# Three PSUM banks for the tiles of the maxima; keys, values and queries share the bank of the turned tiles

## The chip, the cores and the metric

The kernel runs on one core of one Trainium2 chip. The metric is the device time of that core in microseconds (us), the median of several runs. The engines that matter are TensorE (PE in the profile; its weight loads are PEld), VectorE (DVE), ScalarE (ACT), GpSimd (POOL) and SyncE (SP), which here only issues DMAs. PSUM is used as 8 banks of 128 x 512 float32.

## The reference

Cut to what matters; all in float32, B=16 sequences of 128 tokens, D=512.

```python
Q = (layernorm(x) @ Wq + bq)      # 16 heads of 32
K = ctx @ Wk + bk                 # ctx: 2048 x 512 for each sequence, ONE key head of 32
V = ctx @ Wv + bv                 # and one value head of 32
x = x + softmax(Q K^T / sqrt(32)) V @ Wo + bo
x = x + delta_rule_attention(layernorm(x))   # 4 heads of 128, chunks of 64, Ww, Wr, decay
x = x + top1_experts(layernorm(x))           # 16 experts, w1 512x2048, relu, w2 2048x512
```

## The kernel before

The program has two parts. `attention` does the first two lines of work and the routing for all sequences; `experts` then runs the 16 experts. The change is in `attention` alone.

**Iterations and ticks.** `attention` is a pipeline over sequences, with an order written by hand. All engines run the same loop, `for i in range(-1, B + 1): for t in range(TICKS)`, with 128 ticks an iteration. In iteration i, sequence i is scored, sequence i+1 is prepared (`prepare`: normalise x, turn the context, project keys, values and queries) and sequence i-1 is finished (`finish`: output projection, the delta rule with its 6 levels, routing). A tick is no time: it only fixes the program order on each engine. Each engine runs its list strictly in that order, and semaphores tie the lists together. Within a tick PE does the score, then `prepare`, then the weighted sums, then a tile of the maxima, then `finish`; DVE does `prepare`, maxima, `finish`; ACT does the exponential, `prepare`, `finish`.

**The work of an iteration on PE.** A score tile (L370) on every even tick goes to one of two banks, and ACT turns it into weights (L553). The maxima that the softmax subtracts are found ahead, a head group g at a time: 16 tiles (`largest`, L357), each reduced by DVE (L708), then DVE forms the negated maxima (L715), PE turns them (`turn_max`, L362) and ACT copies the row out (L559, `mrow`). The weighted sums are L382. POOL adds up the weights (L917, 15 for each of 4 groups, 60 an iteration), and at tick 9 of the next iteration `sums` (L396) reduces those. From them DVE forms reciprocals (L764) and the attention output `turned` (L767), which the output projection (L336 with wo) waits for at tick 15.

**The work of `prepare`.** DVE takes the statistics of x (L722, L704, at tick NORM), POOL the reciprocal root (L920, L922, same tick), DVE normalises into xin (L727, at tick XN), PE turns xin (L332, at tick XNT), ACT copies it out (L570). 16 tiles of the context are turned by PE (L332, ticks TILE_AT) and copied out by ACT (L582, into cxT, which the trace calls w_first). After every fourth comes the projection of keys and values (L437, ticks KV_AT); ACT copies one half (L589, kvlow), DVE adds the other (L743, kvs) one tick later, ACT rounds the keys (L596) two ticks later, DVE takes the rest (L749). The values are turned at VT_AT. The queries are projected at ticks QPROJ to QPROJ+3 (L414), scaled by DVE (L733), rounded by ACT (L575), the rest taken by POOL (L930), and SP sends them to their place with 12 DMAs of 64 KB (L288, at tick QSEND). The first tile of the maxima of the next sequence (tick 89) waits for all 12.

**Banks.** A_BANK: two for the tiles of the maxima. B_BANK: two for scores. PV_BANK: weighted sums. T_BANK: turned x, context tiles and values. KV_BANK: keys and values, queries, and half of `sums`. P_BANK: `finish`. A use of a bank waits until the use before it has been read.

```python
NORM, XN, XNT, QPROJ, QSEND = 1, 5, 10, 27, 38
TILE_AT = [8 + 4 * k for k in range(KB)]      # 8, 12, ..., 68
MAX_AT, MAX_TURN = [15 * n // 8 - 39 for n in range(KB)], -8   # from tick 32 g of its own iteration
```

Of the kernel before, what the change touches and what calls it, by code (L numbers as in the profile page):

```python
# [9 lines left out]
P = 128  # L10
# [27 lines left out]
NORM, XN, XNT, QPROJ, QSEND = 1, 5, 10, 27, 38  # L38
TILE_AT = [8 + 4 * k for k in range(KB)]
KV_AT = [TILE_AT[4 * c + 3] + 3 for c in range(4)]  # L40
VT_AT = [KV_AT[2 * m + 1] + 7 for m in range(2)]
# [60 lines left out]
def attention(nc, T, w1_first, w1_in):  # L102
    with ExitStack() as ctx:
# [10 lines left out]
        A_BANK, B_BANK, PV_BANK, T_BANK, KV_BANK, P_BANK = bank[0:2], bank[2:4], bank[4], bank[5], bank[6], bank[7]  # L114
# [86 lines left out]
        def level(b, lv, part=0):  # L201
# [6 lines left out]
            [(XNT, ("x", 0))] + [(t, ("t", k)) for k, t in enumerate(TILE_AT)]  # L208
            + [(t, ("v", c)) for c, t in enumerate(VT_AT)])]

# [3 lines left out]
        def turn_read(b, use):  # L214
# [27 lines left out]
        def banks_of(b):  # L242

            return [P_BANK] if b < LAST else [P_BANK, KV_BANK, T_BANK, PV_BANK]
# [81 lines left out]
        def _(e):  # L326
# [33 lines left out]
            def turn_max(b, g):  # L360
                e.wait_ge(*mneg_dve.at(b, g))
                e.transpose(A_BANK[(17 * g + 16) % 2][:, 0:P], mneg[:], ident).then_inc(a_pe.sem, 1)  # L362
# [10 lines left out]
            def weigh(b, u):  # L373
# [3 lines left out]
                if k == 0 and (b or g):  # L377
                    e.wait_ge(*(oS_act.at(b, g - 1) if g else oS_act.at(b - 1, HG - 1)))
# [7 lines left out]
            def sums(b):  # L386
# [12 lines left out]
            def prepare(b, t):  # L399
# [6 lines left out]
                if t == QPROJ:  # L406
                    if b == 0:
                        e.wait_ge(*wq_in.at(0))
                    e.wait_ge(*kvs_dve.at(b, 0))
                    e.wait_ge(*xnT_act.at(b))  # L410
                if QPROJ <= t < QPROJ + HG:
                    cols = slice((t - QPROJ) * P, (t - QPROJ + 1) * P)
                    for c in range(DC):
                        ins = e.matmul(KV_BANK[:, cols], wq[:, c, cols], xnT[:, c, :], start=c == 0, stop=c == DC - 1)  # L414
# [811 lines left out]
```

## Time and profile before

| what | value |
|---|---|
| runs shown | 2424.21 us median of 3 (2420.67 to 2426.93) |
| profiled execution, its own time | 2427.98 us |
| its span (first to last instruction) | 2426.1 us |
| mean granted TensorE clock in it | 0.946 of full speed |
| busy, share of the span | PE 90%, PEld 59%, DVE 57%, ACT 49%, POOL 68% |
| iterations 1 to 14 (with `prepare` and `finish` both) | sums (L396) at 1000.90, 1118.05 and 1236.43 us: 117.8 us apart on average |
| first tile of the maxima | 53.7 us |
| experts | from about 1990 us to the end |

The profile is of one execution, so sums are made against its own time; it lies 3.8 us above the median. An engine's row gives start, duration, engine and line; what stands in square brackets is how long the engine sat idle before, and what ended the idle time. PE records overlap: a matmul's duration includes the draining of the array, so what an instruction costs PE is read from start to next start. Line numbers are those of the kernel before.

### The profile page before, as it was taken

To read this page: it belongs to the slowest core of one execution; us is meant where nothing else is said; L and a number is where in the kernel's file an instruction comes from. 1 tells how busy PE (TensorE), PEld (TensorE's weight loads), DVE (VectorE), ACT (ScalarE), POOL (GpSimd) and SP (SyncE) were. 2 spreads that over 40 slices of the span, in tenths; PEclk is the share of its full clock that TensorE was granted. 3 is DMA by queue.
4 is the path that set the end of the run, shared out by engine and by line. 5 is a ranking of instruction groups with operands and counts; after the bars stand their busy time and mean duration, and the time that the engine had idled before them with its cause. 6 is when DMAs were issued, how large, how long until landed. Compare 5 with 4: busy or idle time off the path is not lost. (4 is left out here: it accounts for less than half of the span.)

```text
span 2426.1 us, 35019 instructions
## 1 busy us (share of the span) xinstructions
PE 2189.4 (90%) x12608; PEld 1429.9 (59%) x12608; DVE 1371.0 (57%) x2311; ACT 1193.3 (49%) x2237; POOL 1638.2 (68%) x1323
## 2 busy tenths in 40 slices
PE   5889898989998989898989898989898769999999
PEld 3435555546464646464646464645554448999998
DVE  2665757566667566666666666666665433333333
ACT  3555554646464646464645455555554313333333
POOL 0676878677777777777777777777777714655655
PEclk9889998999899989998999899989998889999999
DMA  4532120202020202121211111121120009999995
GB/s 160 188 113 66 40 82 24 83 23 83 23 83 23 83 26 80 40 66 40 66 47 58 51 59 63 43 66 42 59 79 9 18 14 375 350 363 346 362 363 189
DMA packets 108157, 263.75 MB, mean 109 GB/s; under 512 B 9849, under 2 KB 35065, under 8 KB 99792
## 3 DMA queue, kind: packets, MB, share of 16 engines
q1 hardware_dynamic: 98448, 235.32, 27.7%
q10 hardware_dynamic: 5952, 14.29, 1.6%
q0 software_dynamic: 3584, 11.90, 1.2%
q8 instruction: 101, 1.65, 0.3%
q14 instruction: 72, 0.59, 0.1%
HBM read 223.74 MB, written 25.72 MB: 103 GB/s over the span
## 5 line engine op out<-in xcount | busy, mean ns | idle before, releaser
L917 POOL TENSOR_TENSOR psum<-psum,p 128x512 f32<-128x512 f32 x896 | 1162.9, 1298 | 291.7 <-ACT p L553 197.7
L708 DVE TENSOR_REDUCE mpart<-bank 128x1 f32<-128x512 f32 x1024 | 675.0, 682 | 403.5 <-PE bank L357 396.1
L553 ACT ACTIVATE p<-bank 128x512 f32<-128x512 f32 x1024 | 596.8, 600 | 553.5 <-PE bank L370 543.6
L357 PE MATMUL bank<-kT,qT 96*128 96x512 f32 x1024 | 484.1, 480 | 62.6 <-DVE mpart L708 32.5
L370 PE MATMUL bank<-qT,kT 97*128 97x512 f32 x1024 | 502.4, 492 | 4.7 <-ACT p L553 4.0
L357 PEld LDWEIGHTS bank<-kT,qT 96*128 96x128 f32 x1024 | 199.6, 196 | 211.5 <-DVE mpart L708 104.6
L370 PEld LDWEIGHTS bank<-qT,kT 97*128 97x128 f32 x1024 | 201.7, 197 | 142.6 <-issue 113.6
L382 PE MATMUL bank<-p,v 128*32 128x512 f32 x2048 | 271.4, 651 | 0.0
L1159 POOL TENSOR_TENSOR w2l<-w,w2h 128x1024 fp32r<-128x1024 f32 x64 | 203.2, 3177 | 75.1 <-PE ebank L1074 54.4
L332 PE MATMUL bank<-cst,w_first 128*128 128x128 f32 x1024 | 164.1, 287 | 21.7 <-DMA w_first<-in_ctx 18.0
L332 PEld LDWEIGHTS bank<-cst,w_first 128*128 128x128 f32 x1024 | 134.3, 149 | 64.9 <-issue 29.4
L917 POOL TENSOR_TENSOR psum<-p 128x512 f32<-128x512 f32 x64 | 81.8, 1278 | 122.5 <-ACT p L553 101.6
L582 ACT COPY w_first<-bank 128x512 f32<-128x512 f32 x256 | 149.3, 586 | 15.0 <-PE bank L332 14.9
L1102 ACT ACTIVATE hh<-ebank 128x512 fp32r<-128x512 f32 x64 | 38.3, 599 | 225.3 <-PE ebank L1058 225.3
L1096 ACT CAST w2h<-w 128x2048 fp32r<-128x2048 f32 x64 | 121.5, 1898 | 44.1 <-DMA w<-in_w 44.1
L382 PEld LDWEIGHTS bank<-p,v 128*32 128x32 f32 x2048 | 56.7, 116 | 141.7 <-issue 107.3
L437 PE MATMUL bank<-w_first,wkv 128*64 128x512 f32 x512 | 125.7, 612 | 10.0 <-ACT w_first L582 9.8
L336 PE MATMUL bank<-wo,turned 128*128 128x512 f32 x128 | 90.3, 799 | 38.8 <-DVE turned L767 38.8
L1058 PE MATMUL ebank<-dT,w_first 128*128 128x128 f32 x1024 | 120.9, 279 | 0.9 <-DVE dT L1117 0.9
L1058 PEld LDWEIGHTS ebank<-dT,w_first 128*128 128x128 f32 x1024 | 120.0, 195 | 2.4 <-issue 1.2
L1123 DVE TENSOR_TENSOR w2l<-w,w2h 128x1024 fp32r<-128x1024 f32 x64 | 79.1, 1236 | 71.9 <-PE ebank L1074 48.0
L1128 DVE SCALAR_TENSOR_TENSOR hl<-ebank,hh 128x512 fp32r<-128x512 f32 x64 | 44.2, 691 | 133.4 <-ACT hh L1102 133.4
(159 smaller groups left out, 3137.8 us busy)
## 6 DMA issues: line engine op xcount, KB each, us to landing
w<-in_w SPq DMA_DIRECT2D x48, 2048.0 KB, 20.1
w_first<-in_ctx SPq DMA_DIRECT2D x64, 1024.0 KB, 4.9
w_first<-in_w SPq DMA_DIRECT2D x16, 2048.0 KB, 11.6
dispatched<-route ACTq DMA_DIRECT2D x17, 513.0 KB, 4.4
dis<-dispatched SPq DMA_DIRECT2D x16, 513.0 KB, 3.5
qT<-qh SPq DMA_DIRECT2D x128, 64.0 KB, 2.0
xin<-in_x SPq DMA_DIRECT2D x16, 256.0 KB, 2.6
qT<-qs SPq DMA_DIRECT2D x64, 64.0 KB, 2.0
```

The source lines that it names most:

```text
L332: ins = e.transpose(out[0:m, j * P:(j + 1) * P], src(j), ident)
L357: e.matmul(a[:], qT[b % 2][0:3 * HD, (4 * g + h) * P:(4 * g + h + 1) * P], kT[b % 2][0:3 * HD, c * 512:(c + 1) * 512], start=True, stop=Tr ...
L370: e.matmul(B_BANK[u % 2][:], kT[b % 2][0:3 * HD + 1, k * P:(k + 1) * P], qT[b % 2][0:3 * HD + 1, g * 512:(g + 1) * 512], start=True, stop= ...
L382: ins = e.matmul(PV_BANK[HD * j:HD * (j + 1), :], v1[b % 2][:, k + j, :], p[(UNITS * b + u + j) % NP][:], start=k == 0, stop=k == KB - 4)
L437: ins = e.matmul(KV_BANK[rows, :], wkv[:, j, :], cxT[c % 2][:, j, :], start=j < 2, stop=j >= 2)
L553: e.activation(p[n % NP][:], B_BANK[u % 2][:], ACT.Exp).then_inc(p_act.sem, 1)
L582: e.copy(cxT[c % 2][:, :, kk * P:(kk + 1) * P], turn_bank(b, ("t", k))[:].rearrange("p (c t) -> p c t", c=DC)).then_inc(cxT_act.sem, 1)
L708: e.tensor_reduce(mpart[g % 2][:, n:n + 1], A_BANK[(17 * g + n) % 2][:], AX.X, ALU.max).then_inc(max_dve.sem, 1)
L917: e.tensor_tensor(acc[:], first[:], p[(UNITS * b + u) % NP][:], ALU.add).then_inc(psum_pool.sem, 1)
L1058: ins = e.matmul(H_BANK[g][:, f * P:(f + 1) * P], w1[q][:, c, (4 * g + f) * P:(4 * g + f + 1) * P], dT[q][:, c, :], start=c == 0, stop=c = ...
L1096: e.copy(w2h[g][:], w2[q][:, 4 * g:4 * g + 4, :]).then_inc(w2h_act.sem, 1)
L1159: e.tensor_tensor(w2l[g % 2][:, 2:4, :], w2[q][:, 4 * g + 2:4 * g + 4, :], w2h[g][:, 2:4, :].bitcast(F32), ALU.subtract).then_inc(w2l_pool ...
```

## The change

KV_BANK is given up: A_BANK gets its bank as a third one, and all that used KV_BANK in `prepare` now takes its turn in T_BANK. `sums` puts its reciprocal half into PV_BANK. `turn_read` gives the wait for the use before. Since T_BANK now has 24 uses an iteration in place of 19, the ticks are laid out anew: context tiles at 9, 12, 15, 18, then 25, 28, 31, 34, and so on up to 66, keys and values at 21, 37, 53, 69, queries at 72 to 75, values at 78 and 81.

```diff
-NORM, XN, XNT, QPROJ, QSEND = 1, 5, 10, 27, 38
-TILE_AT = [8 + 4 * k for k in range(KB)]
+NORM, XN, XNT, QPROJ, QSEND = 0, 3, 6, 72, 82
+TILE_AT = [9 + 16 * (k // 4) + 3 * (k % 4) for k in range(KB)]
 KV_AT = [TILE_AT[4 * c + 3] + 3 for c in range(4)]
-VT_AT = [KV_AT[2 * m + 1] + 7 for m in range(2)]
+VT_AT = [78, 81]
-        A_BANK, B_BANK, PV_BANK, T_BANK, KV_BANK, P_BANK = bank[0:2], bank[2:4], bank[4], bank[5], bank[6], bank[7]
+        A_BANK, B_BANK, PV_BANK, T_BANK, P_BANK = bank[0:3], bank[3:5], bank[5], bank[6], bank[7]
             [(XNT, ("x", 0))] + [(t, ("t", k)) for k, t in enumerate(TILE_AT)]
+            + [(t, ("k", c)) for c, t in enumerate(KV_AT)] + [(QPROJ, ("q", 0))]
             + [(t, ("v", c)) for c, t in enumerate(VT_AT)])]
+            if kind == "q":
+                return q_dve.at(b)
+            if kind == "k":
+                return kvs_dve.at(b, i)
+        def a_bank(b, g, n):
+            return A_BANK[(17 * (4 * b + g) + n) % 3]
             def largest(b, g, n):
-                a = A_BANK[(17 * g + n) % 2]
-                if n >= 2:
-                    e.wait_ge(*max_dve.at(b, 16 * g + n - 2))
-                elif n == 0 and 64 * b + 16 * g >= 1:
-                    e.wait_ge(*max_dve.at(0, 64 * b + 16 * g - 1))
-                elif n == 1 and 4 * b + g >= 1:
-                    e.wait_ge(*mrow_act.at(0, 4 * b + g - 1))
+                group = 4 * b + g
+                a = a_bank(b, g, n)
+                if n >= 3:
+                    e.wait_ge(*max_dve.at(b, 16 * g + n - 3))
+                elif n == 2 and group:
+                    e.wait_ge(*mrow_act.at(0, group - 1))
+                elif group:
+                    e.wait_ge(*max_dve.at(0, 16 * group - 2 + n))
             def weigh(b, u):
-                    e.wait_ge(*(oS_act.at(b, g - 1) if g else oS_act.at(b - 1, HG - 1)))
+                    e.wait_ge(*(oS_act.at(b, g - 1) if g else o_dve.at(b - 1, "recip3")))
             def sums(b):
-                if b + 1 < B:
-                    e.wait_ge(*kvs_dve.at(b + 1, 3))
-                for out, lhs, src in ((KV_BANK, cst[:, C_ONES, 0:HD], psum), (P_BANK, cst[:, C_STACK, 0:HD], oS)):
+                for out, lhs, src in ((PV_BANK, cst[:, C_ONES, 0:HD], psum), (P_BANK, cst[:, C_STACK, 0:HD], oS)):
             def prepare(b, t):
                 if t == QPROJ:
-                    e.wait_ge(*kvs_dve.at(b, 0))
+                    e.wait_ge(*turn_read(b, ("q", 0)))
                 if t in KV_AT:
-                    if c:
-                        e.wait_ge(*kvs_dve.at(b, c - 1))
-                    elif b:
-                        e.wait_ge(*(o_dve.at(b - 2, "recip3") if b > 1 else kvs_dve.at(0, 3)))
-                    if c == 1:
-                        e.wait_ge(*q_dve.at(b))
+                    e.wait_ge(*turn_read(b, ("k", c)))
```

Line numbers below are, for each kernel, its own; L340, L366, L379, L403, L344 and L391 after the change are L332, L357, L370, L396, L336 and L382 before it.

The first place is PE from tick 4 to tick 12 of an iteration, where x is turned (`cst,xin`) and `sums` stands (psum and oS). Before:

```order
L370 MATMUL bank<-qT,kT 128x512
L357 MATMUL bank<-kT,qT 128x512
L370 MATMUL bank<-qT,kT 128x512
L332 MATMUL bank<-cst,w_first 128x128 x4
L357 MATMUL bank<-kT,qT 128x512
L396 MATMUL bank<-psum,cst 32x512 x4
L396 MATMUL bank<-oS,cst 32x512 x4
L357 MATMUL bank<-kT,qT 128x512
L370 MATMUL bank<-qT,kT 128x512
L332 MATMUL bank<-cst,xin 128x128 x4
```

And in the changed kernel, from the score of tick 6:

```order
L379 MATMUL bank<-qT,kT 128x512
L340 MATMUL bank<-cst,xin 128x128 x4
L366 MATMUL bank<-kT,qT 128x512
L379 MATMUL bank<-qT,kT 128x512
L366 MATMUL bank<-kT,qT 128x512
L340 MATMUL bank<-cst,w_first 128x128 x4
L403 MATMUL bank<-psum,cst 32x512 x4
L403 MATMUL bank<-oS,cst 32x512 x4
L366 MATMUL bank<-kT,qT 128x512
```

The turning of x, which stood behind `sums`, now stands ahead of it, and the first context tile directly before `sums`.

The second place is ACT after the first projection of keys and values (kvlow is its copy), up to the copy of the second context tile behind it. Before:

```order
L589 COPY kvlow<-bank 64x512
L611 ACTIVATE rk,ss<-xn 128x128 x4
L553 ACTIVATE p<-bank 128x512
L582 COPY w_first<-bank 128x4x128
L559 CAST mrow<-bank 4x128
L596 CAST kT<-kvs 32x512 x2
L620 COPY turned<-bank 128x512
L553 ACTIVATE p<-bank 128x512
L617 ACTIVATE rk<-xn,rn 128x128 x4
```

In the changed kernel:

```order
L591 COPY kvlow<-bank 64x512
L555 ACTIVATE p<-bank 128x512
L598 CAST kT<-kvs 32x512 x2
L613 ACTIVATE rk,ss<-xn 128x128 x4
L555 ACTIVATE p<-bank 128x512
L561 CAST mrow<-bank 4x128
L584 COPY w_first<-bank 128x4x128
L622 COPY turned<-bank 128x512
L555 ACTIVATE p<-bank 128x512
L619 ACTIVATE rk<-xn,rn 128x128 x4
```

The two casts of the keys, which wait for kvs, now stand ahead of the squares, of an exponential, of the row of maxima and of the tile's copy.

The third place is SP over one iteration: the rows of maxima (mrow), the context loads and the queries (qh, qs). Before:

```order
L279 DMA qT<-mrow 1x4x128
L270 DMA w_first<-in_ctx 128x2048
L288 DMA qT<-qh 32x4x128 x8
L288 DMA qT<-qs 32x4x128 x4
L270 DMA w_first<-in_ctx 128x2048
L279 DMA qT<-mrow 1x4x128
L270 DMA w_first<-in_ctx 128x2048 x2
L279 DMA qT<-mrow 1x4x128
```

In the changed kernel:

```order
L287 DMA qT<-mrow 1x4x128
L278 DMA w_first<-in_ctx 128x2048 x2
L287 DMA qT<-mrow 1x4x128
L278 DMA w_first<-in_ctx 128x2048 x2
L296 DMA qT<-qh 32x4x128 x8
L296 DMA qT<-qs 32x4x128 x4
L287 DMA qT<-mrow 1x4x128
```

The 12 sends have moved from behind the first of the four rows of maxima to directly ahead of the third.

## Rows read from the trace of the kernel before

**Rows 1.** The page: engines, and the costliest groups (mean ns of one after busy us).

```profile
PE 2189.4 (90%) x12608; PEld 1429.9 (59%) x12608; DVE 1371.0 (57%) x2311; ACT 1193.3 (49%) x2237; POOL 1638.2 (68%) x1323
...
L708 DVE TENSOR_REDUCE mpart<-bank 128x1 f32<-128x512 f32 x1024 | 675.0, 682 | 403.5 <-PE bank L357 396.1
L553 ACT ACTIVATE p<-bank 128x512 f32<-128x512 f32 x1024 | 596.8, 600 | 553.5 <-PE bank L370 543.6
```

**Rows 2.** Waits of PE, 12 iterations (409 to 1813 us): total us, times, longest.

```profile
PE bank L336 <- DVE turned L767: 27.7, 12, 2.3
PE bank L357 <- ACT mrow L559: 21.6, 23, 1.2
PE bank L357 <- DVE mpart L708: 20.9, 36, 0.7
...
PE bank L332 <- ACT w_first L582: 5.5, 12, 0.5
```

**Rows 3.** Timeline around `sums` of one iteration: start, duration, [idle before <-releaser].

```profile
1115.47 1.29 POOL L917 TENSOR_TENSOR psum<-psum,p 128x512 f32<-128x512 f32 x1
...
1116.33 0.51 PE L370 MATMUL bank<-qT,kT 97*128 97x512 f32 x1
...
1116.98 0.57 POOL L922 TENSOR_TENSOR rs<-rs,mhalf 128x1 f32<-128x1 f32 x1
...
1117.58 1.52 DVE L727 TENSOR_SCALAR xin<-xin,mv,rs 128x512 f32<-128x512 f32 x1 [0.33 <-POOL rs L922]
...
1118.05 1.07 PE L396 MATMUL bank<-psum,cst 128*32 128x512 f32 x8
...
1120.48 0.60 PE L332 MATMUL bank<-cst,xin 128*128 128x128 f32 x4
...
1121.81 0.66 PE L332 MATMUL bank<-cst,w_first 128*128 128x128 f32 x4 [0.25 <-ACT xnT L570]
...
1126.21 2.07 PE L336 MATMUL bank<-wo,turned 128*128 128x512 f32 x2 [2.31 <-DVE turned L767]
```

**Rows 4.** Windows of 4 us there: busy us of each engine, then PE's granted clock.

```profile
1122.00:1126.00 4.00, 1.42 (x7) 0.68 (x6) 4.00 (x6) 1.34 (x3) 3.39 (x3) 0.91 0.23 68
1126.00:1130.00 4.00, 3.79 (x8) 2.25 (x9) 0.76 (x2) 1.00 (x2) 3.60 (x3) 0.50 0.00 0
```

**Rows 5.** Timeline from the first projection of keys and values, one iteration.

```profile
1019.25 1.94 PE L437 MATMUL bank<-w_first,wkv 128*64 128x512 f32 x8 [0.26 <-ACT w_first L582]
...
1021.23 0.59 ACT L589 COPY kvlow<-bank 64x512 f32<-64x512 f32 x1 [1.54 <-PE bank L437]
...
1021.86 0.74 DVE L743 SCALAR_TENSOR_TENSOR kvs<-bank,bkv,kvlow 64x512 f32<-64x512 f32 x1
...
1023.06 0.60 ACT L553 ACTIVATE p<-bank 128x512 f32<-128x512 f32 x1
...
1024.18 1.25 ACT L596 CAST kT<-kvs 32x512 fp32r<-32x512 f32 x2
...
1024.32 0.49 PE L357 MATMUL bank<-kT,qT 96*128 96x512 f32 x1 [1.24 <-ACT mrow L559]
...
1024.65 1.05 PE L414 MATMUL bank<-xnT,wq 128*128 128x128 f32 x8
...
1026.68 0.60 PE L332 MATMUL bank<-cst,w_first 128*128 128x128 f32 x4
```

**Rows 6.** Sending the queries, its landing, and PE at ticks 76 and 89.

```profile
1032.66 5.21 SPq L288 DMA_DIRECT2D qT<-qh  x8
...
DMA to landing us min/median/max: 2.0/2.0/2.1
...
1072.41 0.39 PE L370 MATMUL bank<-qT,kT 97*128 97x512 f32 x1
...
1082.49 0.47 PE L357 MATMUL bank<-kT,qT 96*128 96x512 f32 x1
```

**Rows 7.** Timeline of the start: the first tile of the maxima.

```profile
53.71 1.19 PE L357 MATMUL bank<-kT,qT 96*128 96x512 f32 x2 [1.44 <-DVE kT L749]
```

More of the change, by code:

```diff
@@ L242, in banks_of @@
         def banks_of(b):
-            return [P_BANK] if b < LAST else [P_BANK, KV_BANK, T_BANK, PV_BANK]
+            return [P_BANK] if b < LAST else [P_BANK, A_BANK[2], T_BANK, PV_BANK]
         block = ctx.enter_context(nc.Block())
@@ L361, in turn_max @@
                 e.wait_ge(*mneg_dve.at(b, g))
-                e.transpose(A_BANK[(17 * g + 16) % 2][:, 0:P], mneg[:], ident).then_inc(a_pe.sem, 1)
+                e.transpose(a_bank(b, g, 16)[:, 0:P], mneg[:], ident).then_inc(a_pe.sem, 1)
             def score(b, u):
@@ L413, in prepare @@
                     for c in range(DC):
-                        ins = e.matmul(KV_BANK[:, cols], wq[:, c, cols], xnT[:, c, :], start=c == 0, stop=c == DC - 1)
+                        ins = e.matmul(turn_bank(b, ("q", 0))[:, cols], wq[:, c, cols], xnT[:, c, :], start=c == 0, stop=c == DC - 1)
                     if t == QPROJ + HG - 1:
@@ L428, in prepare @@
                     e.wait_ge(*cxT_act.at(b, 4 * c + 3))
-                    if c:
-                        e.wait_ge(*kvs_dve.at(b, c - 1))
-                    elif b:
-                        e.wait_ge(*(o_dve.at(b - 2, "recip3") if b > 1 else kvs_dve.at(0, 3)))
-                    if c == 1:
-                        e.wait_ge(*q_dve.at(b))
+                    e.wait_ge(*turn_read(b, ("k", c)))
                     for j in range(DC):
                         rows = slice(64 * (j % 2), 64 * (j % 2) + 2 * HD)
-                        ins = e.matmul(KV_BANK[rows, :], wkv[:, j, :], cxT[c % 2][:, j, :], start=j < 2, stop=j >= 2)
+                        ins = e.matmul(turn_bank(b, ("k", c))[rows, :], wkv[:, j, :], cxT[c % 2][:, j, :], start=j < 2, stop=j >= 2)
                     ins.then_inc(kv_pe.sem, 1)
@@ L558, in max_row @@
                     e.wait_ge(*(mrow_in[g - 2].at(b) if g >= 2 else mrow_in[g + 2].at(b - 1)))
-                e.copy(mrow[g % 2][:], A_BANK[(17 * g + 16) % 2][0:4, 0:P]).then_inc(mrow_act.sem, 1)
+                e.copy(mrow[g % 2][:], a_bank(b, g, 16)[0:4, 0:P]).then_inc(mrow_act.sem, 1)
             def out_sum(b, g):
@@ L588, in prepare @@
                         e.wait_ge(*(kvs_dve.at(b, c - 1) if c else kvs_dve.at(b - 1, 3)))
-                    e.copy(kvlow[half(c), :], KV_BANK[half(c + 1), :]).then_inc(kvlow_act.sem, 1)
+                    e.copy(kvlow[half(c), :], turn_bank(b, ("k", c))[half(c + 1), :]).then_inc(kvlow_act.sem, 1)
                 if t - 2 in KV_AT:
@@ L707, in largest @@
                 e.wait_ge(*a_pe.at(b, 17 * g + n))
-                e.tensor_reduce(mpart[g % 2][:, n:n + 1], A_BANK[(17 * g + n) % 2][:], AX.X, ALU.max).then_inc(
+                e.tensor_reduce(mpart[g % 2][:, n:n + 1], a_bank(b, g, n)[:], AX.X, ALU.max).then_inc(
                     max_dve.sem, 1)
@@ L732, in prepare @@
                         e.wait_ge(*q_in.at(b - 1, 11))
-                    e.scalar_tensor_tensor(heads(qs[:]), heads(KV_BANK[:]), SCALE,
+                    e.scalar_tensor_tensor(heads(qs[:]), heads(turn_bank(b, ("q", 0))[:]), SCALE,
                                            bq[:].unsqueeze(2).to_broadcast([P, DC, P]), ALU.mult, ALU.add).then_inc(
@@ L742, in prepare @@
                         e.wait_ge(*kl_dve.at(b - 1, c + 1))
-                    e.scalar_tensor_tensor(kvs[c // 2][half(c), :], KV_BANK[half(c), :], bkv[half(c), 0:1],
+                    e.scalar_tensor_tensor(kvs[c // 2][half(c), :], turn_bank(b, ("k", c))[half(c), :], bkv[half(c), 0:1],
                                            kvlow[half(c), :], ALU.add, ALU.add).then_inc(kvs_dve.sem, 1)
@@ L763, in finish @@
                     e.wait_ge(*sums_pe.at(b))
-                    e.reciprocal(cut(recip, h), cut(KV_BANK, h)).then_inc(o_dve.sem, 1)
+                    e.reciprocal(cut(recip, h), cut(PV_BANK, h)).then_inc(o_dve.sem, 1)
                 if t == POST["att"]:
```

## The prediction

> **What bounds the kernel now.** I read the page first. PE is busy 90% of the span, no other engine much over two thirds [rows 1], so outside the experts' part time goes where PE waits. The waits of PE over 12 like iterations come next [rows 2]: 27.7 us for `turned` at tick 15, 21.6 us for the row of maxima (mrow), 20.9 us for DVE's reductions (mpart), 5.5 us for the copies of context tiles (w_first). The change can touch the last three, 48.0 us, 4.0 us an iteration; over the 14 iterations with all their work that is 56 us.
>
> Then I read the timeline to see what ends each wait, because a wait of PE is worth its length only if nothing else ends just behind it. Around `sums` it is a chain through four engines [rows 3]: POOL adds its last weights (1115.47), only then makes the reciprocal root for the next sequence's x (1116.98 to 1117.55), DVE normalises x (1117.58 to 1119.10), and PE turns it at 1120.48, 1.4 us after it is ready and 2.4 us behind `sums`. From `sums` (1118.05) a second chain runs through DVE's reciprocals to `turned`, and PE meets it after 2.31 us of idling, at 1126.21. So every tile that PE could do earlier between tick 0 and tick 15 only lengthens that idle time. In the middle of the iteration, behind the first projection of keys and values, PE idles 1.24 us for mrow [rows 5].
>
> **The change, part by part.** All sums are for one iteration from 1 to 14.
>
> *x is turned before `sums` (XNT 10 to 6).* This is the largest term. PE reaches tick 6 at 1116.33 [rows 3], and its score takes some 0.4 us, so it would turn x at about 1116.7. What it turns is ready at 1119.10. NORM and XN are only one and two ticks earlier; POOL's root still stands behind its last addition, and DVE waits for that root already (0.33 us), so xin comes no earlier. PE therefore stands about 2.4 us, and as its list is strict, `sums` stands behind it. From x to `sums` the new list has x, a maxima tile, a score, a maxima tile and context tile 0. x with one tile and one score took 1121.81 - 1120.48 - 0.25 = 1.08 us [rows 3]; for the other two I take 0.7 (an estimate: two of the same three kinds). `sums` starts at 1119.15 + 1.78 = 1120.9, not 1118.05: +2.85, and `turned` follows by as much. If DVE's saved idle moments bring POOL's last addition forward, this falls to about 2.1, and I keep that as the low end. I take +2.8.
>
> *The clock around it.* After the idle time that ends at 1126.21 the granted clock falls from 0.91 of a window to 0.50, which is the lower of the two levels, 1.2 GHz [rows 4]. The new stand before `sums` is about as long, so `sums` and the tiles may run at that level: its two halves take about 1.85 us at full speed (an estimate: two records like the one of 1.07 us, a little overlapped [rows 3]), so up to +1.9. Nothing shows whether the fall lands on them; I take +0.8 and keep 0 and 1.9. The Trainium skill (TensorE: Matmul & The Clock Gate, Part 1: The HAM clock gate) says the low level is the default and activity lifts it; by it a stand can only cost clock. The trace agrees, with 0.50 behind the 2.31 us stand.
>
> *A context tile hidden.* The tile of tick 16 moves to 15, ahead of the wait for `turned`, where PE is idle anyway. A tile is a part of the 1.08 us above, about 0.4, and up to twice that in the slow stretch. I take -0.6.
>
> *Keys and values in the turn bank, first group (23 to 21).* Two things meet here. The last maxima tile of the group now stands behind the projection, so DVE reduces it and forms mneg before it takes kvs; and ACT casts the keys, which wait for kvs, ahead of all else (second place in the change). From the projection's start: 1.9 until the maxima tile, 0.55 until DVE starts, 0.68 reduction, 0.25 for mneg, 0.74 kvs [rows 1, 5]: 4.1 us. Then on ACT the casts 1.25, the squares 1.25 (from 1021.82 to 1023.06), an exponential 0.60, mrow 0.25, the tile's copy 0.6, in all 4.0 [rows 1, 5]. Only then is the bank free for the second context tile: 8.2 us behind the projection's start. Before it took 1026.68 - 1019.25 = 7.43 us to the like tile, with 1.24 of waiting for mrow and with two blocks of queries (0.8 each from 1024.65 [rows 5]) that now go elsewhere, and without one score of 0.3: like for like 6.1. That is +2.1, less the 0.26 waited ahead of the projection, +1.9. So the wait for mrow goes, and a longer one for kvs and ACT's copies comes. Low end 0.3, if ACT is less loaded than my sum; I take +1.9. The Trainium skill (TensorE: Matmul & The Clock Gate, Architectural detail) says ScalarE's queue is strictly first in, first out, TensorE alone pulling weight loads ahead. Were it otherwise, the copy could pass casts and squares and the term would be about -0.6; by the rule the term stands, and rows 5 agree (kvlow, exponential, casts in the list's order).
>
> *The rest of the middle.* Removed: a wait for mpart and one for a copy, about 0.6 and 0.5 with refilling 0.3, together -1.4 [rows 2]. Added: tiles that share one bank 3 ticks apart. A tile may follow 1.33 us behind the one before (1120.48 to 1121.81 [rows 3]); where the three ticks hold nothing of `finish`, PE's own work between is about as long, and ACT's 0.60 exponentials and 1.25 casts lie between. I count six such places an iteration at 0.2 to 0.3 each, 1.5, and 0.2 before the queries. Together +0.3, between -1.4 and +1.5.
>
> *Queries late (27 to 72, sent at 82).* SP needs 5.21 us for 8 sends, so 7.8 for 12, and the last lands 2.0 behind its issue [rows 6]: 9.2 us from the first. DVE's scaling and ACT's rounding come ahead, 1.5 us. Needed: 10.7 from the end of the projection. PE's list from tick 76 to 89 took 1082.49 - 1072.41 = 10.08 us [rows 6], plus 0.4 for the values now at 81, less 0.2 of drain: 10.3. So the first maxima tile waits 0.4. What is queued behind it on PE is everything, scores too. If the sends land later, each us counts in full. I take +0.4, between 0 and 1.5.
>
> *At no cost.* The 16 matmuls of the queries are only moved. The new wait of the weighted sums for the reciprocals at tick 17 lies behind `turned`, which PE has met at 15. mrow at tick 121: its 0.61 us lies directly before a wait for routing, so PE just waits there longer. The mpart waits between ticks 2 and 13 vanish into the stand for x and for `turned`.
>
> **Sum.** 2.8 + 0.8 - 0.6 + 1.9 + 0.3 + 0.4 = +5.6 us an iteration, 78 over 14. The start: before the first maxima tile at 53.7 [rows 7] the queries no longer hide under context loads, perhaps +5 for projecting and sending 12 pieces behind the last keys, less 2 as the first group goes at DVE's 0.68 a tile; iteration 0 and the last save perhaps 4 us of maxima waits. Net about -2 with rounding, +-6. 2428 + 76 = 2504 for an execution like the profiled one, and 3.8 less beside the median: **2500 us**.
>
> **The rivals.**
>
> *Only the stand for x costs.* The middle's new waits are fully paid by the removed ones (1.9 + 0.3 becomes 0, no clock, queries just in time). 14 x 2.8 = 39: 2463. For it: ACT is idle a good part of the time on average, so its lag may be smaller. Against it: rows 5 show ACT and DVE in unbroken work exactly there.
>
> *The clock takes more.* Two stands an iteration of over 2 us (x, and the keys' group with 3.4 us in pieces) each bring a stretch at 1.2 GHz; a further 2 us an iteration, the price of a doubled `sums`, 28 us: 2530. This is the rule named above, at work once more. For it: rows 4. Against it: the wait of 1.24 us did not bring one, so short pieces may not.
>
> *It is faster.* One mechanism: xin is ready when PE reaches tick 6. It decides if POOL's root comes 2.4 us earlier, which needs POOL's last additions that much earlier; then three banks give what they promise in the middle, the waits for mrow and mpart and copies go (1.24 + 0.6 + 0.5 with refilling 0.3 each), some 2.7 us an iteration, 38 in all: 2386. Against it: POOL's list has no gap between the additions at that place, and its order there has not changed.
>
> *No net change.* The bank waits save 2.7, the stand costs 2.8: 2424.
>
> **How the numbers follow.** Forecast 0.47, only the stand 0.20, clock 0.18, faster 0.10, no change 0.05. The predicted time is the forecast's. The range: down to 2445 takes in the single stand; up to 2545 takes in the clock and later landings (0.4 becoming 1.5 is 15 us). Left out are faster, no change and tails, about 0.2. Within 0.3% (7 us) a measurement of this kernel could not tell it from no change. Faster by more: 0.10; within: 0.05; slower: 0.85.
>
> **What would show it.** Right: `sums` rows lie about 123 us apart; PE waits for DVE xin (after the change it is the first reason at the turning of x) some 2.4 us, 14 times; mrow is gone from the list of PE's waits; waits for kvs and for copies of w_first have grown to 2 to 4 us an iteration; a small wait for the DMA of queries at the first maxima tile. Wrong: x turned at once after tick 6's score, or the second context tile less than 7 us behind the first projection. The prediction fails most likely if DVE and POOL run earlier against PE than here: their lead is measured in this order of the work, and a PE that stands more leaves them more time.

## The result, and the profile after

The changed kernel takes 2559.2 us (median of 4 runs, 2548.2 to 2562.5); the kernel before took 2422.7 us beside it (median of 4). The ratio is 1.055 [1.053, 1.058]: 136.5 us slower, where +76 was forecast. The sign and the two places of the new waits were as forecast, the size was outside the range of 2445 to 2545.

The profiled execution of the changed kernel has a time of 2559.62 us of its own. Its page answers to [rows 1]:

```profile
span 2557.8 us, 35006 instructions
...
PE 2247.7 (88%) x12608; PEld 1459.1 (57%) x12608; DVE 1378.5 (54%) x2311; ACT 1193.4 (47%) x2237; POOL 1632.9 (64%) x1323
```

The same 12608 matmuls keep PE busy 58 us longer than before (2247.7 against 2189.4) in a span 132 us longer. PE thus both works more slowly and stands more: 58 us of the difference are slower work, 73 us are idle time. Its waits from 409 to 1813 us, the stretch of [rows 2], now hold 11 iterations (total us, times, longest):

```profile
PE bank L340 <- DVE xin L729: 36.2, 11, 3.7
PE bank L344 <- DVE turned L769: 33.3, 11, 3.0
PE bank L515 <- DVE oh L832: 20.5, 11, 1.9
PE bank L366 <- issue: 20.4, 11, 2.3
PE bank L371 <- DVE mneg L717: 6.5, 11, 0.6
PE bank L379 <- ACT p L555: 6.5, 20, 0.7
PE bank L366 <- DVE mpart L710: 6.3, 16, 0.4
PE bank L340 <- DVE kvs L745: 6.3, 11, 0.9
```

The wait for mrow is gone, that for mpart fell from 20.9 to 6.3 us, and two new ones stand for them: 3.3 us an iteration for x, 1.9 us at the first maxima tile. Together the two new ones are 56.6 us here, more than the 42.5 us that mrow and mpart had. The wait for routing (`oh`, L515) has grown too, from 10.9 to 20.5 us: PE comes there earlier, but `oh` does not, so that part of what the third bank saves is lost again (with the maxima on two banks, below, this wait is 10.6).

Now the same stretch as windows, of the kernel before (first) and of the changed one (second): busy us of PE, PEld, DVE, ACT and POOL, then the granted clock.

```profile
409.00:1813.00 1404.00, 1291.09 (x7269) 769.42 (x7268) 904.77 (x1540) 769.10 (x1557) 1045.40 (x906) 0.96 0.17 56
```
```profile
409.00:1813.00 1404.00, 1248.40 (x6734) 734.65 (x6732) 848.86 (x1442) 712.38 (x1439) 968.60 (x844) 0.92 0.16 50
```

The clock fell from 0.96 to 0.92. As there are only the levels 0.5 and 1.0, 16% of the stretch now ran at the low one and 8% before: some 20 us of each iteration in place of 9. At most half of such time is lost (in the iteration shown next, a maxima tile starts 0.43 us behind a score in the low stretch, at 1067.11, and 0.24 us behind one at 1071.35, at the full clock; and some of the time is idle anyway), so the added low stretches cost up to about 5 us an iteration.

The timeline of the changed kernel around `sums` answers to [rows 3]:

```profile
1063.48 0.57 POOL L924 TENSOR_TENSOR rs<-rs,mhalf 128x1 f32<-128x1 f32 x1
...
1064.08 1.49 DVE L729 TENSOR_SCALAR xin<-xin,mv,rs 128x512 f32<-128x512 f32 x1 [0.91 <-POOL rs L924]
...
1065.62 0.83 PE L340 MATMUL bank<-cst,xin 128*128 128x128 f32 x4 [3.66 <-DVE xin L729]
...
1068.52 1.46 PE L403 MATMUL bank<-psum,cst 128*32 128x512 f32 x8
...
1077.08 2.08 PE L344 MATMUL bank<-wo,turned 128*128 128x512 f32 x2 [3.02 <-DVE turned L769]
```

The chain POOL root, DVE normalising, PE is the predicted one, and `sums` begins 2.90 us behind x (1068.52 - 1065.62), where 1.78 was estimated. The windows there say why the estimate was short (the clock stands behind POOL's busy time):

```profile
1064.00:1067.00 3.00, 1.38 (x6) 1.28 (x7) 2.17 (x3) 0.51 (x1) 1.28 (x2) 0.83 0.00 0
1067.00:1070.00 3.00, 3.00 (x18) 1.30 (x21) 1.30 (x2) 1.26 (x3) 0.00 (x0) 0.60 0.27 93
1070.00:1074.00 4.00, 3.73 (x23) 2.03 (x15) 2.69 (x4) 2.21 (x5) 2.68 (x3) 1.00 0.00 0
1074.00:1077.00 3.00, 0.06 (x1) 0.00 (x0) 3.00 (x6) 0.45 (x1) 2.71 (x3) 0.87 0.00 0
1077.00:1080.00 3.00, 2.92 (x4) 1.51 (x5) 0.62 (x2) 0.38 (x1) 2.42 (x3) 0.50 0.01 3
1080.00:1083.00 3.00, 3.00 (x14) 0.47 (x16) 0.00 (x0) 0.22 (x1) 2.34 (x2) 0.50 0.00 0
```

Around and behind the end of the stand for x the clock is 0.83 and 0.60, over the tiles and the first half of `sums`; it is back at 1.00 by 1070, and the stand for `turned` makes it fall again.

The first group of keys and values answers to [rows 5]:

```profile
1087.23 1.94 PE L439 MATMUL bank<-w_first,wkv 128*64 128x512 f32 x8
...
1090.64 0.74 DVE L745 SCALAR_TENSOR_TENSOR kvs<-bank,bkv,kvlow 64x512 f32<-64x512 f32 x1
...
1091.42 1.26 ACT L598 CAST kT<-kvs 32x512 fp32r<-32x512 f32 x2 [0.94 <-DVE kvs L745]
...
1094.51 0.57 ACT L584 COPY w_first<-bank 128x512 f32<-128x512 f32 x1
...
1095.13 1.11 PE L340 MATMUL bank<-cst,w_first 128*128 128x128 f32 x4
```

From the projection to the second context tile it is 7.90 us (1095.13 - 1087.23), where 8.2 was worked out: kvs, casts, squares, an exponential and the copy one behind the other on DVE and ACT. And the queries, which answer to [rows 6]:

```profile
1147.06 5.20 SPq L296 DMA_DIRECT2D qT<-qh  x8
...
1152.31 2.53 SPq L296 DMA_DIRECT2D qT<-qs  x4
...
1156.34 0.47 PE L366 MATMUL bank<-kT,qT 96*128 96x512 f32 x1 [1.44 <-issue]
```

The sends begin at 1147.06; the last record ends at 1154.84, its send is issued about 0.6 before, and lands 2.0 later, at about 1156.2. PE goes on at 1156.34. So the releaser that the trace calls "issue" is here the queries' DMA: a wait of PE for something that no engine's instruction ends. (In the run with idle time filled, below, the trace names it at the same wait: `DMA qT<-qs`.)

Over 12 like iterations the stretches of PE's list are (means, before and after, in us):

| from, to | before | after |
|---|---|---|
| `sums` to the output projection | 8.16 | 8.85 |
| on to the turning of maxima, tick 24 | 13.41 | 13.03 |
| tick 24 to 56 | 34.26 | 33.51 |
| tick 56 to 88 (after: with the queries) | 26.32 | 29.57 |
| tick 88 to 120 | 22.66 | 25.20 |
| tick 120 to routing | 2.85 | 2.84 |
| routing to the next `sums` | 10.08 | 13.97 |
| whole iteration | 117.74 | 126.97 |

The iteration grew by 9.2 us, where 5.6 was summed: 3.9 of it around x (that stretch now also holds the turning of x itself), 2.5 from tick 88, where the queries are waited for, and 2.5 from tick 24 to 88.

The same can be split into slower work and idle time. The 14 iterations from the first `sums` to the fifteenth hold the same matmuls in both kernels (8509 and 8506 records). Before they took 1649.8 us (174.36 to 1824.17), PE busy 1517.2; after 1770.1 us (186.63 to 1956.70), PE busy 1573.5. So over all 14 an iteration grew by 8.6 us: 4.0 of slower work and 4.6 of idle time. The rest of the 132 us is the start: the first `sums` comes 12.3 us later than before. From the fifteenth `sums` to the end both take the same (601.9 and 601.1 us).

### The profile page after: what moved, and what is told of

Same layout as the page of the kernel before. It is cut to its first block and busy times, and to the rows that moved or that the text cites. A ratio compares the mean times of both kernels' runs of the same rounds, so it can differ in the third digit from the quotient of the medians.

```text
span 2557.8 us, 35006 instructions
## 1 busy us (share of the span) xinstructions
PE 2247.7 (88%) x12608; PEld 1459.1 (57%) x12608; DVE 1378.5 (54%) x2311; ACT 1193.4 (47%) x2237; POOL 1632.9 (64%) x1323
## 5 line engine op out<-in xcount | busy, mean ns | idle before, releaser
L366 PE MATMUL bank<-kT,qT 96*128 96x512 f32 x1024 | 490.8, 483 | 48.9 <-issue 26.6
L379 PE MATMUL bank<-qT,kT 97*128 97x512 f32 x1024 | 513.2, 507 | 13.5 <-ACT p L555 12.3
L366 PEld LDWEIGHTS bank<-kT,qT 96*128 96x128 f32 x1024 | 211.1, 206 | 195.0 <-issue 122.9
L379 PEld LDWEIGHTS bank<-qT,kT 97*128 97x128 f32 x1024 | 206.9, 204 | 156.1 <-issue 104.3
L391 PE MATMUL bank<-p,v 128*32 128x512 f32 x2048 | 269.4, 647 | 0.0
L340 PE MATMUL bank<-cst,w_first 128*128 128x128 f32 x1024 | 171.5, 296 | 15.1 <-DVE kvs L745 9.8
L340 PEld LDWEIGHTS bank<-cst,w_first 128*128 128x128 f32 x1024 | 130.5, 151 | 68.3 <-issue 32.0
L391 PEld LDWEIGHTS bank<-p,v 128*32 128x32 f32 x2048 | 57.1, 117 | 153.4 <-issue 107.1
L344 PE MATMUL bank<-wo,turned 128*128 128x512 f32 x128 | 94.7, 837 | 50.8 <-DVE turned L769 50.8
L1060 PEld LDWEIGHTS ebank<-dT,w 128*128 128x128 f32 x1024 | 117.5, 192 | 1.4
L1060 PE MATMUL ebank<-dT,w 128*128 128x128 f32 x1024 | 118.2, 275 | 0.0
## 6 DMA issues: line engine op xcount, KB each, us to landing
w_first<-in_w SPq DMA_DIRECT2D x16, 2048.0 KB, 12.3
```

The costliest lines, as they stand in the source:

```text
L340: ins = e.transpose(out[0:m, j * P:(j + 1) * P], src(j), ident)
L366: e.matmul(a[:], qT[b % 2][0:3 * HD, (4 * g + h) * P:(4 * g + h + 1) * P], kT[b % 2][0:3 * HD, c * 512:(c + 1) * 512], start=True, stop=Tr ...
L379: e.matmul(B_BANK[u % 2][:], kT[b % 2][0:3 * HD + 1, k * P:(k + 1) * P], qT[b % 2][0:3 * HD + 1, g * 512:(g + 1) * 512], start=True, stop= ...
L391: ins = e.matmul(PV_BANK[HD * j:HD * (j + 1), :], v1[b % 2][:, k + j, :], p[(UNITS * b + u + j) % NP][:], start=k == 0, stop=k == KB - 4)
L1060: ins = e.matmul(H_BANK[g][:, f * P:(f + 1) * P], w1[q][:, c, (4 * g + f) * P:(4 * g + f + 1) * P], dT[q][:, c, :], start=c == 0, stop=c = ...
```

## The experiments

My theory after the result was that the mechanisms of the prediction hold, but that each stand of PE also costs a stretch at 1.2 GHz, and that the two moves in the order (x ahead, queries late) make nearly the whole loss, not the banks. The rival was that the shared bank, with 24 uses in a row, is what costs: then undoing the moves would give back little. Each kernel was timed in 3 rounds beside the kernel before; ratios are to that kernel. Edits are to the changed kernel unless it is said otherwise. "An iteration" means the difference of the medians divided by 14, so it holds a share of the start too; a table behind the experiments parts the start, the slower work and the idle time.

### x back behind `sums`

```diff
-NORM, XN, XNT, QPROJ, QSEND = 0, 3, 6, 72, 82
+NORM, XN, XNT, QPROJ, QSEND = 1, 5, 10, 72, 82
```

> The changed kernel with NORM, XN, XNT back at 1, 5, 10, all else kept: x is turned behind sums again. Theory (the stand for x ahead of sums, with the slow clock it brings, is the largest part): the wait for xin goes and 4 to 5 us an iteration come back, 2485 to 2505 us. Rival (the bank shared by keys, queries and tiles is the cause): under 1.5 us an iteration comes back, 2535 to 2560.

Measured: 2465.0 us, ratio 1.017 [1.015, 1.019]. That is 94 us less than the changed kernel, 6.7 an iteration, and more than my theory had expected (2485 to 2505). The wait for xin is gone, and the clock in the steady stretch is 0.96 again, as in the kernel before:

```profile
409.00:1813.00 1404.00, 1274.47 (x7113) 753.42 (x7112) 896.91 (x1528) 755.37 (x1532) 1024.81 (x892) 0.96 0.16 53
```

The stand itself had 3.3 us, so another 3.4 an iteration went with it. PE's busy time, with the same 12608 matmuls, says what this is:

```profile
PE 2196.8 (89%) x12608; PEld 1431.7 (58%) x12608; DVE 1375.1 (56%) x2311; ACT 1191.8 (48%) x2237; POOL 1631.9 (66%) x1323
```

The changed kernel has 2247.7 us there. Of the 97.6 us between the two spans (2557.8 and 2460.2) 51 are slower work and 47 are idle time. The slower work I had underrated twice, in the prediction (+0.8) and here.

### Queries early again

```diff
-NORM, XN, XNT, QPROJ, QSEND = 0, 3, 6, 72, 82
-TILE_AT = [9 + 16 * (k // 4) + 3 * (k % 4) for k in range(KB)]
+NORM, XN, XNT, QPROJ, QSEND = 0, 3, 6, 24, 35
+TILE_AT = [(9, 30, 45, 60)[k // 4] + 3 * (k % 4) for k in range(KB)]
```

> The changed kernel with the queries projected at ticks 24 to 27 and sent at 35, and the context tiles behind them moved (30, 33, 36, 39, 45, ...), x still turned at tick 6. Theory (the late queries hold the first maxima tile and bring slow clock): 2 to 2.5 us an iteration come back, 2523 to 2535 us. Rival (the sends are hidden but for 0.4 us, as predicted): at most 8 us in all, 2548 to 2560, and the wait at the first maxima tile was of another cause.

Measured: 2499.6 us, ratio 1.031 [1.029, 1.033]: 60 us less than the changed kernel, 4.3 an iteration, and again more than my theory had expected (2523 to 2535). The wait at the first maxima tile is gone. The context tiles move with it, so this is the price of the queries' place together with that of the tiles around it. It is not the length of that wait: 11.4 us of the gain come ahead of the first `sums`, and in the 14 iterations, 3.4 us shorter each, the idle time is the same (14.0 and 13.9), as waits for kvs, xr and Y have come in its place. What has fallen there is the time at 1.2 GHz, from 19.7 to 14.6 us an iteration, and with it PE's busy time, by 3.3.

### Both back, the banks kept

```diff
-NORM, XN, XNT, QPROJ, QSEND = 0, 3, 6, 72, 82
-TILE_AT = [9 + 16 * (k // 4) + 3 * (k % 4) for k in range(KB)]
+NORM, XN, XNT, QPROJ, QSEND = 1, 5, 10, 24, 35
+TILE_AT = [(9, 30, 45, 60)[k // 4] + 3 * (k % 4) for k in range(KB)]
```

> Both of the above: x turned at tick 10 again, queries at 24 to 27. Theory (the two stands are nearly all of the loss): 2450 to 2475 us if the first group's wait for kvs stays as predicted (1.9 us an iteration), 2420 to 2440 if the queries behind the first projection hide that one too. Rival (shared bank): 2500 or more.

Measured: 2428.9 us, ratio 1.000 [0.999, 1.002]. So with the new banks, x behind `sums` and the queries behind the first projection again, nothing measurable is lost. The single moves give back 94 and 60, both together 130: each is worth less once the other is undone. The rival, that the shared bank makes the loss, has fallen. The time is the one expected for a hidden wait for kvs, but that condition did not come: PE waits 22.4 us for kvs (L421 and L340) in 12 iterations, 1.9 each. The number was luck in that. The new banks are not free either: the 42.5 us of waits for mrow and mpart in [rows 2] are gone, but in the same stretch there are those 22.4 for kvs, and xr has 20.5 where it had 7.8, Y 15.0 where it had 6.3, `oh` 20.5 where it had 10.9.

### The maxima on two banks

```diff
-            return A_BANK[(17 * (4 * b + g) + n) % 3]
+            return A_BANK[(17 * (4 * b + g) + n) % 2]
...
-                if n >= 3:
-                    e.wait_ge(*max_dve.at(b, 16 * g + n - 3))
-                elif n == 2 and group:
-                    e.wait_ge(*mrow_act.at(0, group - 1))
+                if n >= 2:
+                    e.wait_ge(*max_dve.at(b, 16 * g + n - 2))
+                elif n == 0 and group:
+                    e.wait_ge(*max_dve.at(0, 16 * group - 1))
                 elif group:
-                    e.wait_ge(*max_dve.at(0, 16 * group - 2 + n))
+                    e.wait_ge(*mrow_act.at(0, group - 1))
```

> The changed kernel with the tiles of the maxima going round two banks again (the third lies idle), everything else kept. Theory (a third bank buys little, since other waits end just behind): 0 to 2 us an iteration slower than the changed kernel, 2559 to 2590 us. Rival (the third bank is worth the 3 to 4 us an iteration of mpart and mrow waits): 2600 us or more.

Measured: 2588.8 us, ratio 1.067 [1.065, 1.069], 29.6 us more than the changed kernel. The third bank alone is worth 2.1 us an iteration, in a kernel where the stands for x and for queries swallow part of what it saves. The waits from 409 to 1813 us, 11 iterations, show that as well:

```profile
PE bank L366 <- DVE mpart L710: 41.2, 52, 1.2
...
PE bank L366 <- ACT mrow L561: 25.2, 33, 1.6
PE bank L340 <- DVE xin L729: 24.6, 11, 2.3
```

mpart and mrow are back, and the stand for x is 2.2 us an iteration in place of 3.3.

### The old kernel with x early

Here the edit is to the kernel before; its banks and all its other ticks stay.

```diff
-NORM, XN, XNT, QPROJ, QSEND = 1, 5, 10, 27, 38
+NORM, XN, XNT, QPROJ, QSEND = 0, 3, 6, 27, 38
```

> The kernel before with one part of the change alone: NORM, XN, XNT at 0, 3, 6 in place of 1, 5, 10. Banks and all other ticks as before. Theory (the stand for x ahead of sums stems from this part alone and needs no shared bank): 4.5 to 7 us an iteration slower, 2490 to 2520 us, and the clock falls from 0.946 to about 0.925. Rival (it needs the shared bank or the third bank, since these let PE run ahead): under 2450 us.

Measured: 2497.6 us, ratio 1.030 [1.029, 1.032], 74 us more (5.3 an iteration) than the same kernel with x behind `sums`. Its waits from 409 to 1813 us, 12 iterations:

```profile
PE bank L357 <- DVE mpart L708: 38.4, 47, 1.4
PE bank L336 <- DVE turned L767: 27.7, 12, 2.3
PE bank L332 <- DVE xin L727: 24.9, 12, 2.3
```

This tests the first term by itself. The stand is 2.1 us an iteration here, near the 2.4 predicted, and not 3.3: with two banks PE still loses its time to mpart (38.4 us, against 20.9 in [rows 2]) and reaches tick 6 later. In the changed kernel the third bank took those waits away, so PE came to the same chain earlier; the run before, with a stand of 2.2 us on two banks, says that this is what lengthened it. The price is again over the stand's length. Of 4.7 us that the 14 iterations grew by each, 3.2 are idle time, the stand and 1.5 more of waiting for mpart; 1.5 are slower work. The clock in this stretch is 0.93, against 0.96:

```profile
409.00:1813.00 1404.00, 1253.43 (x6888) 737.35 (x6888) 872.50 (x1485) 730.22 (x1479) 999.70 (x871) 0.93 0.16 52
```

### Idle time filled with matmuls that nobody needs

The changed kernel, with 16 more transposes on PE ahead of the wait for x, and 10 ahead of the first maxima tile. Their results are never read; nothing is left out. (The condition on b and the waits on v_act and ohloc keep them off banks that are still read.)

```diff
+                if n == 0 and g == 0 and b:
+                    e.wait_ge(*v_act.at(b, 1))
+                    for _ in range(10):
+                        e.transpose(T_BANK[:, 0:P], ident, ident)
                 if n == 0:
...
+                if t == XNT and b >= 2:
+                    if b >= 3:
+                        e.wait_ge(*post_dve.at(b - 3, "ohloc"))
+                    for _ in range(16):
+                        e.transpose(P_BANK[:, 0:P], ident, ident)
```

> The changed kernel with matmuls added that nobody reads, in the two stands of PE: 16 turnings of the identity into an idle bank directly before the wait for xin (iterations 1 to 14), 10 before the first tile of the maxima of a sequence. At full speed they take about 1.5 and 0.9 us, less than the stands (3.5 and 1.7 us), so they cost nothing there. Theory (part of the loss is the slow clock that the stands bring): the mean clock rises from 0.92 to 0.93 or more and 1 to 3 us an iteration come back, 2515 to 2545 us. Rival (the clock follows something else, the stands cost only their length): clock 0.92, 2555 to 2575 us.

Measured: 2527.6 us, ratio 1.044 [1.041, 1.046]: 31.5 us less than the changed kernel, with more work on PE. Its order is unchanged, and nothing in it makes x come earlier, so I put this down to the clock. Two views show it, the windows around the stand for x:

```profile
1049.00:1052.00 3.00, 1.40 (x13) 1.16 (x11) 2.08 (x3) 0.28 (x1) 2.88 (x4) 1.00 0.44 175
1052.00:1055.00 3.00, 2.62 (x19) 1.58 (x23) 2.14 (x4) 1.67 (x3) 0.00 (x0) 1.00 0.25 87
```

and PE's timeline there:

```profile
1048.82 1.58 PE L415 MATMUL bank<-cst 128*128 128x128 f32 x13
1052.31 0.66 PE L340 MATMUL bank<-cst,xin 128*128 128x128 f32 x4 [1.91 <-DVE xin L738]
...
1054.29 1.06 PE L407 MATMUL bank<-psum,cst 128*32 128x512 f32 x8
```

PE idles 1.91 us and not 3.66, the clock stays at 1.00, and `sums` comes 1.98 us behind x where it came 2.90. Over the 14 iterations the time at 1.2 GHz is 14.1 us each and no longer 19.7. The Trainium skill (TensorE: Matmul & The Clock Gate, Part 1: The HAM clock gate) has activity lifting the clock and idleness dropping it; this run agrees, 0.936 over the span against 0.920. So 2.25 us an iteration is a lower bound of the clock's share at the two places together, since other low stretches remain. The second wait now carries the name of the DMA:

```profile
PE bank L370 <- DMA qT<-qs: 12.1, 11, 2.0
```

### Queries in the middle

```diff
+NORM, XN, XNT, QPROJ, QSEND = 1, 5, 10, 56, 66
+TILE_AT = [(9, 25, 41, 62)[k // 4] + 3 * (k % 4) for k in range(KB)]
```

> The changed kernel with x at tick 10 and the queries at ticks 56 to 59, sent at 66, the last four context tiles behind them (62 to 71). The sends end well before the first tile of the maxima. Theory (only lateness of the queries costs, and as they fill a stretch where PE waits for DVE in the delta rule's levels they may do better than at tick 24): the wait at the first maxima tile is gone, 2405 to 2435 us. Rival (queries at 24 to 27 were good because they cover ACT's and DVE's late work behind the first projection, the 1.9 us of the prediction): 2440 to 2460 us.

Measured: 2447.1 us, ratio 1.009 [1.008, 1.011], 18 us more than with the queries at 24 to 27. The projection is early enough here to be waited for by nobody, and the time is the rival's. The rival's reason is not what the traces show, though: PE idles less here than with the queries at 24 to 27 (9.5 us an iteration against 10.8), so no cover is missed. What is higher is the time at 1.2 GHz, 13.6 us an iteration against 11.0, and PE's busy time, by 2.3 with the same matmuls. Half of what PE works in the added low stretches is 1.3 us an iteration (an estimate), about the size of the whole loss. Why this order has more of such stretches was not tried.

### Keys and values behind the last maxima tile

The first group is spaced so that its projection, three ticks behind the fourth tile, stands behind the last maxima tile of the head group; the later tiles move by one tick.

```diff
+NORM, XN, XNT, QPROJ, QSEND = 1, 5, 10, 25, 36
+TILE_AT = [9, 12, 15, 19] + [(31, 46, 61)[k // 4] + 3 * (k % 4) for k in range(12)]
```

> The kernel with x at tick 10 and early queries (2428.9 us), and the first projection of keys and values moved from tick 21 to 22, so that the last tile of the maxima stands ahead of it on PE and DVE reduces it while the projection runs; queries at 25 to 28, later tiles one tick later. Theory (kvs is late in the first group because DVE takes that reduction and mneg first, 0.85 us): PE's wait for kvs before the queries falls from 1.4 us to under 1, and 0.4 to 0.8 us an iteration come back, 2417 to 2424 us. Rival (kvs waits for kvlow anyway): no change, 2426 to 2432.

Measured: 2403.1 us, ratio 0.992 [0.990, 0.993]: 26 us less than with both moves undone, and more than the 6 to 11 expected. So something else had been moved by the same edit. The next run takes the shift of the later tiles alone:

```diff
+NORM, XN, XNT, QPROJ, QSEND = 1, 5, 10, 24, 35
+TILE_AT = [(9, 31, 46, 61)[k // 4] + 3 * (k % 4) for k in range(KB)]
```

> The kernel with x at 10 and queries at 24 (2428.9 us), whose first projection stays at tick 21, but whose later context tiles stand one tick later (31, 46, 61), as in the kernel that measured 2403.1 us. It parts the two differences of that one. Theory (the gain of 26 us came from DVE's reduction no longer standing ahead of kvs): 2424 to 2432 us here. Rival (it came from where the later tiles stand against the delta rule's levels, whose waits fell from 25 to 10 us): 2403 to 2412 us.

Measured: 2412.0 us, ratio 0.995 [0.993, 0.997]. Of the 26 us, 17 come from the later tiles being one tick later, and 9 from the first projection being behind the last maxima tile, with the queries one tick later. (By the ratios it is 14 and 8, each uncertain by about 6, as the runs were timed beside different runs of the kernel before.) And one more tick:

```diff
+NORM, XN, XNT, QPROJ, QSEND = 1, 5, 10, 25, 36
+TILE_AT = [9, 12, 15, 19] + [(32, 47, 62)[k // 4] + 3 * (k % 4) for k in range(12)]
```

> The kernel of 2403.1 us with its later context tiles one tick later still (32, 47, 62). If the place of the tiles against the levels sets the time, this moves it by more than 5 us either way; if only the first projection does, it stays at 2400 to 2407 us.

Measured: 2396.1 us, ratio 0.988 [0.986, 0.990]. It is the fastest version, 1.2% faster than the kernel before and 6.4% faster than the changed one, with the same banks. Waits of PE from 409 to 1813 us (12 iterations), with both moves undone (first) and in this version (second):

```profile
PE bank L490 <- DVE xr L804: 20.5, 24, 1.5
...
PE bank L421 <- DVE kvs L745: 16.8, 12, 1.7
PE bank L348 <- DVE Y L796: 15.0, 24, 1.0
...
PE bank L340 <- DVE kvs L745: 5.6, 12, 0.5
```
```profile
PE bank L340 <- DVE kvs L745: 15.7, 24, 0.8
PE bank L421 <- DVE kvs L745: 12.2, 12, 1.0
PE bank L490 <- DVE xr L804: 8.8, 24, 0.5
PE bank L340 <- ACT w_first L584: 8.7, 23, 0.5
...
PE bank L348 <- DVE Y L796: 3.7, 12, 0.3
```

The waits inside the delta rule (L490 for xr, L348 for Y) shrank by 23 us: the context tiles now stand where PE waited for DVE between two levels. The waits for kvs (L340) grew by 10. This is the gain of the first tick (there xr has 7.8 and Y 9.2 already). The last tick is not explained by it: Y fell by 5.6 us more, kvs (L340) rose by 7.6, and 2.4 of the 7 us come ahead of the first `sums`.

### All runs, start and iterations

Each row is read from that run's trace. The start is the first row of `sums`; the rest is the mean of the 14 iterations from there to the fifteenth `sums`. All but the filled kernel hold the same matmuls there (8506 to 8509 records), so more busy time means slower work. Idle time is length less busy time. Time at 1.2 GHz is an estimate, 2 x (1 - clock) added up over 400 windows of each trace.

| kernel | start, us | iteration | PE busy | PE idle | at 1.2 GHz |
|---|---|---|---|---|---|
| before | 174.4 | 117.8 | 108.4 | 9.5 | 10.6 |
| before, x early | 178.9 | 122.5 | 109.9 | 12.7 | 15.0 |
| changed | 186.6 | 126.4 | 112.4 | 14.0 | 19.7 |
| maxima on two banks | 190.9 | 128.5 | 112.6 | 15.9 | 19.9 |
| idle time filled | 185.9 | 124.2 | 112.8 | 11.4 | 14.1 |
| queries early | 175.3 | 123.1 | 109.1 | 13.9 | 14.6 |
| x late | 180.7 | 119.9 | 109.0 | 11.0 | 10.7 |
| both back | 170.3 | 118.5 | 107.7 | 10.8 | 11.0 |
| queries in the middle | 169.1 | 119.6 | 110.0 | 9.5 | 13.6 |
| later tiles one tick later | 172.0 | 116.9 | 107.2 | 9.7 | 9.1 |
| projection behind the last maxima tile too | 171.0 | 116.5 | 107.0 | 9.5 | 8.4 |
| and one more tick | 168.6 | 116.2 | 106.7 | 9.5 | 8.6 |

A matmul record's end is modelled, so a difference of busy times is good to about 1 us an iteration only.

## Why the prediction came out as it did

**What bounds the kernel, and the removed waits: right.** mrow left the list, mpart fell to 6.3 us. The third bank is worth 2.1 us an iteration, shown by taking it away.

**The clock: the step that failed.** Of the +5.6 us an iteration 0.8 was for the clock and 4.8 for all that makes PE stand. Measured over the 14 iterations it is 4.0 of slower work and 4.6 of idle time. So the idle time was right in sum, though single waits were not, and the clock was priced at a fifth of what it cost, which is twice its high end of 1.9. The term counted only the two halves of `sums` as lying in the low stretch behind the stand for x. But x and the tiles behind it run at that level too, and the iteration as a whole has 19.7 us at 1.2 GHz in place of 10.6. A check from the other side: PE's work in those stretches grew by 111 us over the 14 iterations, half of it is 55 us, and its busy time grew by 56. Filling the idle time gave 2.25 us an iteration back without shortening any chain. Taking x back is worth 6.5 us in each of the 14 iterations with the new banks, 3.4 of it slower work, and 4.7 with the old ones, 1.5 of it slower work.

**x ahead of `sums`: right mechanism, sizes short.** The wait stands where it was put, behind the same chain. Its length was taken as 2.4 us from PE's lead over DVE in the order before; it is 3.3. The text named this risk with the wrong sign: it feared that a PE that stands more gives DVE and POOL more time, while the waits removed elsewhere brought PE there earlier. With two banks for the maxima the stand is 2.1 in the old kernel and 2.2 in the changed one, which shows that the working was right for the order it was read from. From x to `sums` it is 2.90 us in the iteration shown, where 1.78 was estimated; with the clock at 1.00 it is 1.98.

**Queries late: right mechanism, size wrong.** The wait was forecast as 0.4 with a high end of 1.5, and is 1.9. The sends and their landing cost what was said, but DVE's scaling and ACT's rounding ahead of them took 2.0 us and not 1.5 (1145.05, where PE goes on behind the projection, to 1147.06). PE's list in between was shorter too: 10.08 us in [rows 6], 9.5 in an iteration of the changed kernel (1271.80 to 1281.33, where the idle time begins), although it now holds both halves of the values and not one. The list of before held waits of 0.22 us for Y and 0.44 for xr there, which are gone.

**First group of keys and values: right in length, wrong in the waits it named.** It is 7.90 us where 8.2 was worked out. From the output projection to tick 88 the table of stretches gives +2.1 us, where 1.9 and 0.3 were summed. But the waits for kvs and for copies of w_first did not grow to 2 to 4 us an iteration: they are 9.3 us over 11 iterations, 0.8 each. The time of the group lies also in waits for mneg and xn, and in the clock, which falls to 0.78 and 0.50 behind 1091.

**The start: wrong in sign.** It was forecast as -2 us and is +12.3. The first maxima tile is at 56.0 us, before 53.7 [rows 7], where about 5 was given; but from there to the first `sums` it takes 10 us more, where savings of 6 us were expected (4 of them for iteration 0 and the last together). The same two moves act in iteration 0: the first `sums` is at 180.7 us with x late, at 175.3 with the queries early, at 170.3 with both.

**The account of the miss.** The profiled execution took 2559.6 us where 2504 was summed for one like it. Of these 56 us about 45 are the clock, 14 the start, and -3 the idle time.

**The rivals.** "The clock takes more" (2530) was nearest and had the right cause, but its further 2 us an iteration were too small, and it left the start as it was. "Only the stand" (2463) falls. "Faster" falls by its own condition: xin was not ready at tick 6. The last version does reach 2396 us, with x left behind `sums` and the context tiles moved. How much of that the new banks give is not shown, since neither that order on two banks for the maxima nor such tiles in the old kernel were run.

**Left open.** Why the iterations of the changed kernel vary from 123 to 129 us, where the kernel before has 117.1 and 118.3 in turn, was not tried; the low stretches do not fall on the same instructions in each. Nor is it known which of the low stretches follows which stand: the 31.5 us given back by filling belong to two places, and only one kernel filled them.

## What to carry to other kernels

An instruction moved forward in an engine's strict order is paid by everything behind it if its operand comes through a chain on other engines. Read when that chain ends, and price the move with the waits that the same change removes, as they bring the engine to the spot earlier. Then add the clock, over the whole iteration and not only for the instructions just behind the stand: x early cost 3.4 us an iteration of slower work beside a stand of 3.3, and 1.5 beside one of 2.1. PE's busy time at an equal number of matmuls shows this part directly. A change that joins new resources with a new order should be timed as two; here the third bank was worth 30 us, and two moves in the order lost 130.

## What the hardware showed that was not expected

A stand of 3.66 us left the clock at 0.83 and 0.60 in the windows around and behind its end, one of 1.91 us with useless transposes ahead of it did not (1.00 in both), and adding 26 small matmuls to most iterations made the kernel 31.5 us faster. Leaving PE with more to do can be the cheaper choice where it must wait in any case; one kernel shows it here, and its stand of 3.02 us for `turned`, which was not filled, still brought the clock to 0.57.
